# First-layernorm statistics of the next query block computed inside the output-projection loop, on VectorE, in an eight-core transformer layer

## The chip, the cores and the metric

The kernel runs on all 8 cores of one Trainium2 chip. Each core takes one half of the token groups of one of four sequences (2048 of 4096 tokens) and never speaks to another core. The metric is the device time in microseconds (us) of the slowest core.

## What is computed

One pre-norm layer on x of shape (4, 4096, 2048): attention with 16 query heads over 4 key/value heads of 128, then a gated feed-forward part of inner width 6144 with weights rounded to fp8.

```python
def _layernorm(x, axis=-1, eps=1e-5):
    m = jnp.mean(x, axis=axis, keepdims=True)
    v = jnp.var(x, axis=axis, keepdims=True)
    return (x - m) / jnp.sqrt(v + eps)
# attention, on x = layernorm(x)
q = _rmsnorm((x @ Wq).reshape(b, s, H, DH), q_gamma)
k = _rmsnorm((x @ Wk).reshape(b, s, KVH, DH), k_gamma)
v = (x @ Wv).reshape(b, s, KVH, DH)
scores = jnp.einsum('bqhd,bkhd->bhqk', q, k) * DH ** (-0.5)      # causal
out = jnp.einsum('bhqk,bkhd->bqhd', softmax(scores), v) @ Wo + x
# the layer
x = x + attention(_layernorm(x))
x = x + ffn(_layernorm(x))   # silu(x @ gate * s) * (x @ up * s) @ down * s
```

## The kernel before

Everything lies transposed: the 2048 features are 16 tiles of 128 partitions (`DC = FC = 16`), the tokens are columns, 512 at a time. The kernel has three stages. First the keys and values of all 4096 tokens are made in eight steps of 512. Then a loop over four query blocks (`for qc in range(NQC)`) does all of attention for 512 queries. Then the feed-forward part runs in two halves of 1024 tokens.

The change touches the query-block loop. One block goes through these steps:

1. **Statistics of the first layernorm** (lines 475 to 500). ScalarE copies each of the 16 feature tiles of `xtt` (fp32) to `xnn` (bf16); TensorE multiplies each by a column of ones (`ones1`) and accumulates the sum over features in row 0 of the PSUM bank `PS_G`; ScalarE then squares each tile of `xnn` in place; TensorE accumulates the squares in `PS_H`. `t_sumsq` is the semaphore count of the last matmul.
2. **Rows and normalisation** (from line 501). VectorE makes mean and variance rows, ScalarE the inverse deviation, TensorE spreads both over 128 partitions, and VectorE normalises the 16 tiles into `xnn`. The first row operation also waits for `gd["rows1"]` (line 502): the small transfers that stored the previous block's rows, since it overwrites them.
3. **Attention**, eight head pairs.
4. **Output projection** (`for fc in range(FC)`, lines 830 to 879). For each of 16 output tiles: GpSimd issues the transfer of 512 KB of `wo` into one of two buffers `wofc`, and that issue waits for the matmuls that read the buffer two steps earlier; TensorE does 16 matmuls into bank `PS_S0` or `PS_S1`; TensorE then does two statistics matmuls of the *second* layernorm for the step before (`ln2_stats(fc - 1)`), from `qraw` and `qsq`; VectorE adds the two residuals (`rlB`, then `x1t`), casts to `qraw` and squares to `qsq`; SyncE stores `x1t`, and loads the next block's tile of `xtt` over the one just used (the list `preload`), on a semaphore of its own, `X{fc}`.
5. **Rows of the second layernorm** (from line 880), which end with two small stores `rbc<-rowb` on semaphore `RW`.

Each engine takes its instructions strictly in the order in which the Python emits them, and waits are emitted by hand as counts of semaphores. `vop` and `act` also make each VectorE or ScalarE operation wait for the one before on the same engine. All operations are recorded under the line of their helper: matmuls L112, ScalarE L124, VectorE L132, transfers L93.

Of the kernel before, what the change touches and what calls it, by code (L numbers as in the profile page):

```python
# [12 lines left out]
AF = mybir.ActivationFunctionType  # L13
ALU = mybir.AluOpType
# [3 lines left out]
DC = 16  # L18
S = 4096
# [5 lines left out]
NQC = 4  # L25
# [11 lines left out]
def _build():  # L37
# [36 lines left out]
    def wait(e, c, v):  # L74
        assert v <= cnt[c], f"wait on future: {e} {c} {v} > {cnt[c]}"
        if v <= 0:
            return
        emit(e, lambda eng, s=c, v=v: eng.wait_ge(sem[s], v))

    def gwait(e, g):  # L80
        if not g:
            return
        if isinstance(g, list):
            for gg in g:
                wait(e, gg[0], gg[1])
        else:
            wait(e, g[0], g[1])
# [17 lines left out]
    def mm(o, l, r, st, sp, inc=False):  # L105
        if inc:
            cnt["T"] += 1
            emit("tensor", lambda eng, o=o, l=l, r=r, st=st, sp=sp:
                 eng.matmul(o, l, r, start=st, stop=sp).then_inc(sem["T"], 1))
            return cnt["T"]  # L110
        emit("tensor", lambda eng, o=o, l=l, r=r, st=st, sp=sp:
             eng.matmul(o, l, r, start=st, stop=sp))  # L112

    def act(o, i, f, bias=None, scale=None, inc=False):
        kw = {}
        if bias is not None:
            kw["bias"] = bias
        if scale is not None:
            kw["scale"] = scale
        if cnt["S"] > 0:  # L120
            emit("scalar", lambda eng, v=cnt["S"]: eng.wait_ge(sem["S"], v))
        cnt["S"] += 1
        emit("scalar", lambda eng, o=o, i=i, f=f, kw=kw:
             eng.activation(out=o, in_=i, func=f, **kw).then_inc(sem["S"], 1))  # L124
        return cnt["S"]
# [18 lines left out]
    def tinc():  # L144
        cnt["T"] += 1
        last = prog["tensor"].pop()
        emit("tensor", lambda eng, f=last: f(eng).then_inc(sem["T"], 1))
        return cnt["T"]
# [21 lines left out]
    with ExitStack() as TOP:  # L170
# [8 lines left out]
        ones1 = TOP.enter_context(nc.sbuf_tensor("ones1", [128, 1], BF16))  # L179
# [9 lines left out]
        def row(i):  # L189
            return rowb[0:1, i * 512:(i + 1) * 512]  # L190

        ps = [TOP.enter_context(nc.psum_tensor(f"ps{i}", [128, 512], F32))
              for i in range(4)]
# [30 lines left out]
        with ExitStack() as SA:  # L224
# [209 lines left out]
            with ExitStack() as SA2:  # L434
# [27 lines left out]
                minv2_slot = {}  # L462

                preload = [None]
                for qc in range(NQC):
                    K_QC = 8 * qc + 8
                    if preload[0] is not None:
                        xls = preload[0]
                    else:
                        xls = []  # L470
                        for dc in range(DC):
                            xls.append(dma("sync", xtt[:, dc * 512:(dc + 1) * 512],
                                           xq[:, qc * 512:(qc + 1) * 512].rearrange(
                                               "(dc p) t -> p dc t", p=128)[:, dc, :], f"X{dc}"))
                    s_cp = []
                    for dc in range(DC):
                        wait("scalar", f"X{dc}", xls[dc])
                        if dc == 0:
                            gwait("scalar", gd.get("xnn_sq"))
                        s_cp.append(act(xnn[:, dc * 512:(dc + 1) * 512],  # L480
                                        xtt[:, dc * 512:(dc + 1) * 512], AF.Copy))
                    tsx = []
                    for dc in range(DC):
                        wait("tensor", "S", s_cp[dc])
                        if dc == 0:
                            gwait("tensor", gd.get("av10"))
                            gwait("tensor", gd.get("av11"))
                        mm(ps[PS_G][0:1, :], ones1[:, :], xnn[:, dc * 512:(dc + 1) * 512],
                           dc == 0, dc == DC - 1)
                        tsx.append(tinc())  # L490
                    s_sq = []
                    for dc in range(DC):
                        wait("scalar", "T", tsx[dc])
                        s_sq.append(act(xnn[:, dc * 512:(dc + 1) * 512],
                                        xnn[:, dc * 512:(dc + 1) * 512], AF.Square))
                    for dc in range(DC):
                        wait("tensor", "S", s_sq[dc])
                        mm(ps[PS_H][0:1, :], ones1[:, :], xnn[:, dc * 512:(dc + 1) * 512],
                           dc == 0, dc == DC - 1)
                    t_sumsq = tinc()  # L500
                    wait("vector", "T", t_sumsq)
                    gwait("vector", gd.get("rows1"))
                    vop("tensor_scalar", row(R_MEAN), ps[PS_G][0:1, :], 1.0 / D, None, ALU.mult)
# [314 lines left out]
                    def ln2_stats(i):  # L818
                        wait("tensor", "V", v_x1b_of[i])
                        if i == 0:  # L820
                            gwait("tensor", gd.get("lbank0"))
                            gwait("tensor", gd.get("lbank1"))
                        mm(ps[PS_L0][0:1, :], ones1[:, :], qraw[0][:, :], i == 0, i == FC - 1)
                        mm(ps[PS_L1][0:1, :], ones1[:, :], qsq[:, :], i == 0, i == FC - 1)
                        t_st = tinc()
                        gd["qsq"] = ("T", t_st)
                        gd["qraw0"] = ("T", t_st)
                        return t_st

                    for fc in range(FC):  # L830
                        wb_ = fc % 2
                        gwait("gpsimd", gd.get(f"wofc{wb_}"))
                        wod = dma("gpsimd", wofc[wb_][:, :],
                                  wo[:, fc * 128:(fc + 1) * 128].rearrange("(dc p) f -> p dc f", p=128),
                                  f"WO{wb_}")
                        b = PS_S0 if fc % 2 == 0 else PS_S1
                        wait("tensor", f"WO{wb_}", wod)
                        if fc == 0:
                            wait("tensor", "V", v_evall)
                        gwait("tensor", gd.get(f"sbank{fc % 2}"))  # L840
                        for dc in range(DC):
                            mm(ps[b][:, :], wofc[wb_][:, dc * 128:(dc + 1) * 128],
                               attno[:, dc * 512:(dc + 1) * 512], dc == 0, dc == DC - 1)
                        t_wo = tinc()
                        if fc >= 1:
                            ln2_stats(fc - 1)
                        wait("vector", "T", t_wo)
                        gwait("vector", gd.get(f"x1t{fc % 2}"))
                        if fc == 0:
                            wores = []  # L850
                            gwait("vector", gd.get("rlB0"))
                        wores.append(vop("tensor_tensor", rlB[0][:, :], ps[b][:, :],
                                         xtt[:, fc * 512:(fc + 1) * 512], ALU.add))
                        v_x1 = vop("tensor_tensor", x1t[fc % 2][:, :], rlB[0][:, :],
                                   xnn[:, fc * 512:(fc + 1) * 512], ALU.add, inc=True)
                        gd[f"sbank{fc % 2}"] = ("V", v_x1)
                        gwait("vector", gd.get("qraw0"))
                        vop("tensor_copy", qraw[0][:, :], x1t[fc % 2][:, :])
                        gwait("vector", gd.get("qsq"))
                        v_x1b = vop("tensor_tensor", qsq[:, :], qraw[0][:, :], qraw[0][:, :],  # L860
                                    ALU.mult, inc=True)
                        v_x1b_of[fc] = v_x1b
                        wait("sync", "V", v_x1)
                        spd = dma("sync", x1s[fc, :, qc * 512:(qc + 1) * 512],
                                  x1t[fc % 2][:, :], f"SP{fc % 2}")
                        gd[f"x1t{fc % 2}"] = (f"SP{fc % 2}", spd)
                        gd[f"wofc{wb_}"] = ("T", t_wo)
                        if fc == FC - 1:
                            gd["rlB0"] = ("V", v_x1)
                        if qc < NQC - 1:  # L870
                            if fc == 0:
                                preload[0] = []
                            wait("sync", "V", wores[fc])
                            preload[0].append(dma(
                                "sync", xtt[:, fc * 512:(fc + 1) * 512],
                                xq[:, (qc + 1) * 512:(qc + 2) * 512].rearrange(
                                    "(dc p) t -> p dc t", p=128)[:, fc, :], f"X{fc}"))
                        else:
                            preload[0] = None
                    ln2_stats(FC - 1)  # L880
                    t_ln2 = cnt["T"]
                    wait("vector", "T", t_ln2)
# [280 lines left out]
```

## Time and profile before

| what | us |
|---|---|
| median of three timed runs | 6364.97 |
| the three runs | 6345.15, 6364.97, 6578.1 |
| the profiled execution | 6212.52 |
| span of its slowest core (core 7) | 6210.7 |
| spans of its eight cores | 6179.1 to 6210.7 |

The profile is of one execution, on the slowest core. Times in it are from the start of the span. An instruction's row gives start and duration; a bracket gives how long the engine was idle before it and what ended that. The granted clock of TensorE (`PEclk`) is given as a share of its full 2.4 GHz, so 0.50 is 1.2 GHz. The profiled execution is 152 us shorter than the median of the timed runs.

### The profile page before, as it was taken

How to read it: one execution, taken by the hardware profiler on the slowest of the kernel's cores; microseconds unless marked ns; L12 is line 12 of the kernel's file. 1: busy time of each engine (PE TensorE's matmuls, PEld its weight loads, DVE VectorE, ACT ScalarE, POOL GpSimd, SP SyncE). 2: the span in 40 equal slices, each digit the busy share in tenths (PEclk: the TensorE clock that was granted, in tenths of full speed). 3: DMA queues.
4: the chain of work that ended last, by engine and by line, in shares of the span. 5: the costliest groups of instructions: out<-in, count | busy, mean ns of one | idle time of the engine just before them, and what ended most of it. 6: DMA issues, size and time to landing. Idle time of an engine off the chain costs nothing.

```text
span 6210.7 us, 56932 instructions; the slowest of 8 cores (6179.1 to 6210.7 us)
## 1 busy us (share of the span) xinstructions
PE 4538.3 (73%) x16536; PEld 1582.6 (25%) x16536; DVE 1671.6 (27%) x3095; ACT 1698.6 (27%) x2511; POOL 294.1 (5%) x231
## 2 busy tenths in 40 slices
PE   4556545665666656666567777659999999999998
PEld 1112111111111211111111111224444344444443
DVE  2433334433333333333233333331110211111000
ACT  3232323321444225555145556100100000100000
POOL 0000000000000000000100000100000010000000
PEclk8666556566776868788778778879999999999999
DMA  4212121145120531010711100565566996565786
GB/s 89 55 29 53 28 48 21 21 47 75 14 28 1 81 48 14 7 14 7 109 14 14 15 7 1 75 92 39 37 41 41 112 102 53 38 41 35 52 79 70
DMA packets 670616, 271.18 MB, mean 44 GB/s; under 512 B 541286, under 2 KB 611942, under 8 KB 670318
## 3 DMA queue, kind: packets, MB, share of 16 engines
q0 software_dynamic: 598576, 147.86, 32.0%
q1 hardware_dynamic: 71742, 119.68, 7.3%
q8 instruction: 146, 2.39, 0.2%
q14 instruction: 152, 1.25, 0.1%
HBM read 532.77 MB, written 33.57 MB: 91 GB/s over the span
## 4 chain that ended last, share of the span: by engine, by line
PE 54%; ACT 17%; DVE 13%; DMA 7%; issue 7%; DVEq 1%; ACTq 1%; SPq 1%; POOLq 0%
PE ps L112 41%; PE lacc L112 13%; ACT pbt L124 9%; DMA wofc<-wo 4%; ACT xnn L124 4%; ACT rowb L124 3%; DVE pbt L132 2%; DVE rowb L132 2%; DVE xnn L132 2%; DVE xtmp L132 1%; ACT rlrow L124 1%; DVE rlB L132 1%; DMA dbuf<-dw 1%; DMA x1f<-x1s 1%; DVE outt L132 1%
## 5 line engine op out<-in xcount | busy, mean ns | idle before, releaser
L124 ACT ACTIVATE pbt<-ps,biasB,rall 128x512 bf16<-128x512 f32 x1280 | 995.0, 777 | 792.2 <-PE ps L112 419.4
L112 PE MATMUL ps<-pbt,vtok 128*128 128x512 bf16 x1280 | 598.4, 468 | 486.1 <-DVE pbt L132 241.4
L112 PE MATMUL ps<-xn,gbuf 128*128 128x512 bf16 x3072 | 699.0, 381 | 75.7 <-DVE xn L132 75.7
L112 PE MATMUL lacc<-fuse,dbuf 128*128 128x512 bf16 x3072 | 695.9, 390 | 67.4 <-DVE outt L132 58.1
L112 PE MATMUL ps<-xn,ubuf 128*128 128x512 bf16 x3072 | 694.4, 379 | 0.0
L112 PE MATMUL ps<-qhat,khat 128*128 128x512 bf16 x1280 | 609.8, 480 | 5.8 <-DVE qhat L132 5.8
L124 ACT ACTIVATE gact<-ps,gs_sb 128x512 bf16<-128x512 f32 x192 | 131.9, 687 | 1588.4 <-PE ps L112 1588.4
L132 DVE SCALAR_TENSOR_TENSOR fuse<-ps,us_sb,gact 128x512 bf16<-128x512 f32 x192 | 144.2, 751 | 1177.7 <-PE ps L112 1177.6
L112 PE MATMUL ps<-attno,wofc 128*128 128x512 bf16 x1024 | 296.8, 456 | 181.1 <-DMA wofc<-wo 169.6
L112 PEld LDWEIGHTS lacc<-fuse,dbuf 128*128 128x128 fp8e4 x3072 | 305.1, 100 | 458.1 <-issue 119.0
L132 DVE TENSOR_TENSOR pbt<-pbt 128x512 bf16<-128x512 bf16 x640 | 272.3, 426 | 544.1 <-ACT pbt L124 516.7
L112 PEld LDWEIGHTS ps<-xn,gbuf 128*128 128x128 fp8e4 x3072 | 301.6, 98 | 442.1 <-issue 82.7
L112 PEld LDWEIGHTS ps<-xn,ubuf 128*128 128x128 fp8e4 x3072 | 300.6, 98 | 362.5
L112 PEld LDWEIGHTS ps<-pbt,vtok 128*128 128x128 bf16 x1280 | 128.0, 100 | 1001.6 <-issue 981.1
L112 PE MATMUL ps<-xnn,wqhg 128*128 128x512 bf16 x1024 | 274.6, 421 | 74.3 <-DVE xnn L132 74.3
L132 DVE TENSOR_TENSOR pbt<-pbt,mask_sb 128x512 bf16<-128x512 bf16 x512 | 217.8, 425 | 305.7 <-ACT pbt L124 292.9
L112 PE MATMUL lacc<-pbt,ones 128*1 128x512 bf16 x640 | 289.5, 452 | 7.3 <-DVE pbt L132 7.2
L112 PE MATMUL ps<-xnn,wk_sb 128*128 128x512 bf16 x512 | 177.5, 477 | 148.9 <-DVE xnn L132 148.9
L124 ACT ACTIVATE rowb<-rowb,epsb 1x1 f32<-1x1 f32 (+1 forms) x80 | 30.3, 379 | 717.9 <-DVE rowb L132 717.9
L112 PE MATMUL lacc<-xnn,ones 128*1 128x512 bf16 x256 | 149.6, 584 | 83.1 <-ACT xnn L124 39.0
L112 PEld LDWEIGHTS ps<-attno,wofc 128*128 128x128 bf16 x1024 | 111.5, 113 | 365.5 <-issue 297.1
L132 DVE SCALAR_TENSOR_TENSOR outt<-lacc,ds_sb,x1g 128x512 f32<-128x512 f32 x64 | 48.1, 751 | 530.9 <-PE lacc L112 527.2
(97 smaller groups left out, 2760.1 us busy)
## 6 DMA issues: line engine op xcount, KB each, us to landing
xtt<-xT SPq DMA_DIRECT2D x128, 256.0 KB, 3.7
wqhg<-wq POOLq DMA_DIRECT2D x32, 1024.0 KB, 10.0
wofc<-wo POOLq DMA_DIRECT2D x64, 512.0 KB, 9.8
gbuf<-gw POOLq DMA_DIRECT2D x48, 512.0 KB, 9.7
ubuf<-uw POOLq DMA_DIRECT2D x48, 512.0 KB, 13.9
dbuf<-dw POOLq DMA_DIRECT2D x32, 768.0 KB, 21.5
xtt<-xq SPq DMA_DIRECT2D x64, 256.0 KB, 8.0
x1s<-x1t SPq DMA_DIRECT2D x64, 256.0 KB, 6.5
```

The costliest lines, as they stand in the source:

```text
L112: eng.matmul(o, l, r, start=st, stop=sp))
L124: eng.activation(out=o, in_=i, func=f, **kw).then_inc(sem["S"], 1))
L132: getattr(eng, n)(*a, **kw).then_inc(sem["V"], 1))
```

## The change

For query blocks 1 to 3 the statistics of the first layernorm are no longer computed at the head of the block. They are computed inside the output projection of the block before, one feature tile per step: the tile `dc = fc - 2` at step `fc` from 2 on, and tiles 14 and 15 after the loop, ahead of the last `ln2_stats`. The copy and the square move from ScalarE to VectorE. Each tile is done as one chain: VectorE copy, TensorE sum, VectorE square, TensorE sum of squares, emitted behind all else of the step. Block 0 keeps the old code.

```diff
                 preload = [None]
+                xst = {}
...
-                    s_cp = []
-                    for dc in range(DC):
-                        wait("scalar", f"X{dc}", xls[dc])
...
-                    t_sumsq = tinc()
+                    if "t_sumsq" in xst:
+                        t_sumsq = xst.pop("t_sumsq")
+                    else:
+                        (the removed lines, indented)
...
+                    def mk_xstat(dc):
+                        def fn():
+                            wait("vector", f"X{dc}", preload[0][dc])
+                            v_cp = vop("tensor_copy", xnn[:, dc * 512:(dc + 1) * 512],
+                                       xtt[:, dc * 512:(dc + 1) * 512], inc=True)
+                            wait("tensor", "V", v_cp)
+                            if dc == 0:
+                                gwait("tensor", gd.get("av10"))
+                                gwait("tensor", gd.get("av11"))
+                            mm(ps[PS_G][0:1, :], ones1[:, :],
+                               xnn[:, dc * 512:(dc + 1) * 512], dc == 0, dc == DC - 1)
+                            t_s = tinc()
+                            wait("vector", "T", t_s)
+                            v_sq = vop("tensor_tensor", xnn[:, dc * 512:(dc + 1) * 512],
+                                       xnn[:, dc * 512:(dc + 1) * 512],
+                                       xnn[:, dc * 512:(dc + 1) * 512], ALU.mult, inc=True)
+                            wait("tensor", "V", v_sq)
+                            mm(ps[PS_H][0:1, :], ones1[:, :],
+                               xnn[:, dc * 512:(dc + 1) * 512], dc == 0, dc == DC - 1)
+                            xst["t_sumsq"] = tinc()
+                        return fn
+                    xstat_cls = ([mk_xstat(dc) for dc in range(DC)]
+                                 if qc < NQC - 1 else [])
                     for fc in range(FC):
...
+                        if fc >= 2 and xstat_cls:
+                            xstat_cls.pop(0)()
+                    while xstat_cls:
+                        xstat_cls.pop(0)()
                     ln2_stats(FC - 1)
```

## Rows read from the trace of the kernel before

**Rows 1.** The page: busy time, then shares of the chain that ended last.

```profile
PE 4538.3 (73%) x16536; PEld 1582.6 (25%) x16536; DVE 1671.6 (27%) x3095; ACT 1698.6 (27%) x2511; POOL 294.1 (5%) x231
...
PE ps L112 41%; PE lacc L112 13%; ACT pbt L124 9%; DMA wofc<-wo 4%; ACT xnn L124 4%; ACT rowb L124 3%; DVE pbt L132 2%; DVE rowb L132 2%; DVE xnn L132 2%; DVE xtmp L132 1%; ACT rlrow L124 1%; DVE rlB L132 1%; DMA dbuf<-dw 1%; DMA x1f<-x1s 1%; DVE outt L132 1%
```

**Rows 2.** Windows: sum, busy us (count) of PE, PEld, DVE, ACT, POOL; PEclk, DMA, GB/s.

```profile
1346.40:1465.30 118.90, 73.75 (x252) 25.91 (x252) 29.11 (x53) 0.00 (x0) 15.99 (x14) 0.80 0.96 122
...
2092.90:2202.60 109.70, 73.03 (x252) 25.86 (x252) 29.07 (x52) 0.00 (x0) 16.18 (x14) 0.81 0.96 132
2202.60:2246.00 43.40, 20.72 (x38) 3.14 (x36) 11.76 (x18) 23.46 (x37) 0.00 (x0) 0.55 0.18 39
...
2951.50:3058.80 107.30, 70.45 (x252) 25.27 (x252) 29.09 (x53) 0.00 (x0) 16.17 (x14) 0.83 0.97 136
```

**Rows 3.** TensorE's timeline in the projection: two groups of block 1, one of block 3.

```profile
2099.54 3.63 PE L112 MATMUL ps<-attno,wofc 128*128 128x512 bf16 x16
...
2108.55 5.18 PE L112 MATMUL ps<-attno,wofc 128*128 128x512 bf16 x16 [4.86 <-DMA wofc<-wo]
...
4022.88 5.30 PE L112 MATMUL ps<-attno,wofc 128*128 128x512 bf16 x16 [3.56 <-DMA wofc<-wo]
```

**Rows 4.** The same view: three groups of block 0.

```profile
1346.41 5.66 PE L112 MATMUL ps<-attno,wofc 128*128 128x512 bf16 x16 [10.42 <-DMA wofc<-wo]
...
1382.38 6.44 PE L112 MATMUL ps<-attno,wofc 128*128 128x512 bf16 x16 [5.35 <-DMA wofc<-wo]
...
1461.41 3.61 PE L112 MATMUL ps<-attno,wofc 128*128 128x512 bf16 x16 [3.21 <-DMA wofc<-wo]
```

**Rows 5.** Chain of work in order of time, block 0: start us, us, what.

```profile
1446.88 14.28 DMA wofc<-wo
```

**Rows 6.** Timeline from the last projection matmuls of block 1 into block 2.

```profile
2199.64 2.75 PE L112 MATMUL ps<-attno,wofc 128*128 128x512 bf16 x12
...
2202.64 0.69 DVE L132 TENSOR_TENSOR rlB<-ps,xtt 128x512 f32<-128x512 f32 x1 [1.53 <-PE ps L112]
...
2204.23 0.43 DVE L132 CAST qraw<-x1t 128x512 bf16<-128x512 f32 x1
2204.61 0.38 SPq L93 DMA_DIRECT2D xtt<-xq  x1
2204.76 0.42 DVE L132 TENSOR_TENSOR qsq<-qraw 128x512 bf16<-128x512 bf16 x1
2205.33 0.38 PE L112 MATMUL lacc<-qraw,ones 128*1 128x512 bf16 x1 [2.41 <-DVE qsq L132]
2205.55 0.38 PE L112 MATMUL lacc<-qsq,ones 128*1 128x512 bf16 x1
2206.17 1.46 DVE L132 TENSOR_SCALAR rowb<-lacc 1x512 f32<-1x512 f32 x2 [0.98 <-PE lacc L112]
...
2210.88 11.44 ACT L124 ACTIVATE xnn<-xtt 128x512 bf16<-128x512 f32 x16
...
2234.91 1.46 DVE L132 TENSOR_SCALAR rowb<-ps 1x512 f32<-1x512 f32 x2 [23.27 <-PE ps L112]
```

**Rows 7.** Tile `xtt` in block 0's projection: time from issue to landing.

```profile
DMA to landing us min/median/max: 5.8/8.7/11.7
```

**Rows 8.** Timeline after the last block: rows, small stores, who waits.

```profile
4036.04 1.46 DVE L132 TENSOR_SCALAR rowb<-lacc 1x512 f32<-1x512 f32 x2 [0.98 <-PE lacc L112]
...
4043.86 1.14 POOL L93 DMA_DIRECT2D gbuf<-gw  x1 [23.37 <-DMA rbc<-rowb]
```

**Rows 9.** Windows, columns of rows 2: attention, then a wait of the projection.

```profile
1109.00:1111.50 2.50, 1.18 (x4) 0.26 (x4) 1.88 (x5) 1.55 (x3) 0.00 (x0) 1.00 0.88 88
1112.00:1116.00 4.00, 2.72 (x6) 0.42 (x6) 0.85 (x2) 1.38 (x4) 0.00 (x0) 0.50 1.16 135
...
1457.80:1461.40 3.60, 0.40 (x2) 0.02 (x1) 2.24 (x4) 0.00 (x0) 0.00 (x0) 1.00 1.29 148
```

**Rows 10.** Tile `xnn`: the statistics matmuls of the boundaries, min/median/max ns.

```profile
L112 PE MATMUL ps<-xnn,ones x128: 582/585/586, 845.6 to 3090.2; 128*1 128x512 bf16 x128
```

More of the change, by code:

```diff
@@ L474, in _build @@
                                                "(dc p) t -> p dc t", p=128)[:, dc, :], f"X{dc}"))
-                    s_cp = []
-                    for dc in range(DC):
-                        wait("scalar", f"X{dc}", xls[dc])
[L478 to L499, printed above, removed]
-                    t_sumsq = tinc()
+                    if "t_sumsq" in xst:
+                        t_sumsq = xst.pop("t_sumsq")
+                    else:
+                        s_cp = []
+                        for dc in range(DC):
+                            wait("scalar", f"X{dc}", xls[dc])
+                            if dc == 0:
+                                gwait("scalar", gd.get("xnn_sq"))
+                            s_cp.append(act(xnn[:, dc * 512:(dc + 1) * 512],
+                                            xtt[:, dc * 512:(dc + 1) * 512], AF.Copy))
+                        tsx = []
+                        for dc in range(DC):
+                            wait("tensor", "S", s_cp[dc])
+                            if dc == 0:
+                                gwait("tensor", gd.get("av10"))
+                                gwait("tensor", gd.get("av11"))
+                            mm(ps[PS_G][0:1, :], ones1[:, :], xnn[:, dc * 512:(dc + 1) * 512],
+                               dc == 0, dc == DC - 1)
+                            tsx.append(tinc())
+                        s_sq = []
+                        for dc in range(DC):
+                            wait("scalar", "T", tsx[dc])
+                            s_sq.append(act(xnn[:, dc * 512:(dc + 1) * 512],
+                                            xnn[:, dc * 512:(dc + 1) * 512], AF.Square))
+                        for dc in range(DC):
+                            wait("tensor", "S", s_sq[dc])
+                            mm(ps[PS_H][0:1, :], ones1[:, :], xnn[:, dc * 512:(dc + 1) * 512],
+                               dc == 0, dc == DC - 1)
+                        t_sumsq = tinc()
@@ L828, in ln2_stats @@
                         return t_st
+                    def mk_xstat(dc):
[4 more added lines that the diff above has]
+                            wait("tensor", "V", v_cp)
+                            if dc == 0:
+                                gwait("tensor", gd.get("av10"))
+                                gwait("tensor", gd.get("av11"))
+                            mm(ps[PS_G][0:1, :], ones1[:, :],
[12 more added lines that the diff above has]
+                                 if qc < NQC - 1 else [])
                     for fc in range(FC):
```

## The prediction

> **What bounds the kernel now.** I read the page first [rows 1]. TensorE is busy 73% of the span, and the chain that ended last runs mostly over it; the reader should note two smaller entries of that chain, the weight transfer `wofc<-wo` with 4% and ScalarE's `xnn` with 4%. The second is what the change removes for blocks 1 to 3, the first is the place where it puts the work. So the stage table comes next [rows 2]: in the projection ScalarE does nothing, VectorE is busy 29 us of 110 to 119, the DMA share is 0.96, and TensorE is busy only about two thirds. At the boundary between blocks ScalarE is the busiest engine and TensorE sees a clock of 0.55. Then the timelines: what paces the projection [rows 3 to 5], and what happens between the last projection matmul and the next block's rows [rows 6].
>
> The projection goes in pairs. Both buffers are refilled at about the same time, so two groups of 16 matmuls run back to back and then TensorE waits 3.6 to 10.4 us for weights. A group that starts after such a wait takes 5.2 to 6.4 us, since its first matmuls run at 1.2 GHz; the one behind it takes 3.63 us at 2.4 GHz [rows 3, 4]. Block by block, from the third group's first matmul to the last group's residual add, that is 118.9, 109.7 and 107.3 us for 13 steps plus one group, in sum 335.9 us [rows 2], or 8.2 to 9.1 us a step. TensorE's order of work is free of VectorE here: `ln2_stats` is one step late on purpose, so nothing waits for the add, cast and square of the same step.
>
> **What the change removes.** Copies, 32 matmuls and squares run from ScalarE's first copy at 2210.88 to VectorE's first row operation at 2234.91 [rows 6]. From the last residual add (2202.64) to that row operation it is 32.3 us; the other two boundaries have the same operations, and I price them alike.
>
> **What it adds in each step.** The new chain of a step sits in TensorE's queue ahead of the next 16 projection matmuls, and its first link sits in VectorE's queue behind the four operations of the step. So TensorE now waits each step for VectorE to work through the step just ended. From the end of a group, with durations of [rows 6]: 0.24 us to the residual add (2202.64 less the group's end at 2199.64 + 2.75); 2.54 us for add, add, cast and square (2202.64 to 2204.76 + 0.42); 0.11 us gap; the copy, priced as the cast of fp32 to bf16 of that size, 0.43; 0.15 to TensorE (2205.18 to 2205.33); matmul 0.38; 0.24 back (2205.55 + 0.38 to 2206.17); square 0.43; 0.15; and 0.22 until the next matmul can follow. Sum 4.89 us. The two new matmuls can run at the lower clock, 0.585 us each as at the boundaries [rows 10], which adds up to 0.4; I take half, so 5.1 us. Before, the two `ln2_stats` matmuls took 0.4 us at this place [rows 9]. I find no cover for this on TensorE itself: all projection matmuls stand behind it. The only cover is that TensorE was waiting for weights anyway.
>
> Are the weights still the limit? The issue for step fc+2 still goes out at the end of group fc. Landing took up to 14.3 us in block 0 [rows 5]. Until group fc+2 can start there now pass two stalls and a group, 5.1 + 5.2 + 5.1 = 15.4 us. So the transfer falls wholly under the new waits, and a step costs the stall plus the group. Its length then hangs on the clock. Between two groups TensorE has about 0.4 us of `ln2_stats`, 2.9 us of nothing, and two lone matmuls 0.8 us apart. The rows show both outcomes nearby: 3.6 us with 0.40 us of work kept the clock at 1.00, and the group behind took 3.61 us [rows 4, 9]; 3.56 and 4.86 us of waiting lost it [rows 3]; and in attention the clock fell to 0.50 though TensorE had been busy 1.18 us of the 2.5 before [rows 9]. The thin stretch here is about 5 us from dense work to dense work, on the far side of those, so I take a restart at 1.2 GHz in each step, and for the group 5.2 us, the size of the groups behind the shortest waits that lost the clock (5.18 and 5.30 [rows 3]). A step is 5.2 + 5.1 = 10.3 us. The two first groups of a block carry no chain and stay. Thirteen steps plus a group and 0.24: 139.3 us, three times 417.9, against 335.9: **82 us lost**. The bounds: with the clock held, 3.63 + 4.89 = 8.52 us a step, three times 114.6 = 343.9 us, 8 us lost; with the longest restart (6.44 [rows 4]) and both small matmuls slow, 6.44 + 5.3 = 11.7 us a step, 13 x 11.74 + 6.7 = 159.3 us, three times 478, 142 us lost.
>
> On this point the Trainium skill speaks against the change: "TensorE: Matmul & The Clock Gate", in the section on how oscillation of the clock bites real kernels, describes a kernel whose bursts of matmuls are parted by short waits and which starts every burst at the half clock. By it each group would restart slowly, as in my sum; the case that the clock holds would then be out. The trace agrees for the waits of 3.56 us and more and does not for the one of 3.21 us.
>
> **What is left at the boundary.** Chains 13, 14 and 15 follow the last group. Chain 13 and 14 end on VectorE about 6 us behind the residual add. Chain 15 needs tile 15 of `xtt`, whose load is issued 1.97 us behind the add [rows 6] and lands 8.7 us later, 5.8 to 11.7 [rows 7]. So a new wait of some 4 us stands in VectorE's queue; behind it stand the rows of both layernorms. Copy at 10.7, then 0.43 + 0.15 + 0.38 + 0.24 + 0.43 + 0.15 to the last sum of squares at 12.5, `ln2_stats(15)` 0.22 later, and 0.84 more to the first row operation (2205.33 to 2206.17): 13.6, with slow matmuls 14.0. Before it was 3.5. Next the second layernorm's rows, and behind them the wait of line 502 for the small stores, which the old statistics hid: at the end of the last block first row operation to stores landed is 7.8 us [rows 8]. The first layernorm's rows start at 14.0 + 7.8 = 21.8 us instead of 32.3: **10.5 us saved** per boundary, 32 in all. With loads at 5.8 or 11.7 us it is 40 or 23 in all. If neither the load nor the stores were in the way it would be more, but both are plain in the code. Moving work from ScalarE to VectorE costs nothing else: ScalarE has nothing else at either place, VectorE's busy share in the projection goes from a quarter to a third. The weight transfer of the next block's first heads is issued one step ahead of the loop's end and now gets more time, not less.
>
> **Sum.** 82 lost less 32 saved: 50 us slower. On the profiled execution 6212.5 + 50 = 6262.5. The median of the timed runs lies 152 us above it, and I carry the difference over: 6365 + 50 = **6415 us**, 0.8% slower.
>
> **Rivals.**
> *The clock holds.* If the two lone matmuls keep the clock at 1.00, a step is 8.52 us, 8 us are lost and 32 saved: 24 us faster, 6341 us. The 3.6 us stretch of [rows 9] speaks for it, the attention stretch against. The sign turns where a step costs 9.1 us with a group of 4.2 us (13 x 9.1 + 4.4, three times, is 335.9 + 32), less than any group behind a wait of 3.56 us or more. Chance 0.15.
> *The step is longer than I think.* Restarts of 6.44 us, or weights that land later than the 15.4 us of cover (14.28 us is near it), give 11.7 us a step: 142 lost, 23 saved, 119 us slower, 6484 us. Groups around 6 us are common after long waits, which speaks for it; that the waits here are short speaks against it. Chance 0.15.
> *The stall stays hidden and the boundary gives all it seems to.* The statistics go from the path, and only the stores remain: rows start at 3.5 + 7.8 = 11.3 instead of 32.3, 63 us faster, 6302 us. It needs TensorE's in-order queue and tile 15's load not to matter; the load alone speaks against it. Chance 0.03.
> The forecast has 0.65; 0.02 is left for what I don't see.
>
> A difference of 2%, 127 us, is about what a measurement of this kernel can tell from no change. The forecast and the clock rival are well within; of the long-step case about half would pass it. Slower by over 2%: 0.09; faster by over 2%: 0.02; within: 0.89. The range reaches to the two middle rivals, 6335 to 6485 us; the forecast's own is 6385 to 6450.
>
> **What would show it.** In the projection of blocks 0 to 2: steps even instead of paired, 10 to 10.5 us apart; the group's idle time before it ended by `xnn` or PE's own queue, no longer by `wofc<-wo`; PEclk lower than 0.80 in the windows of [rows 2]; groups of 5 to 6 us. The last block's projection unchanged. At the boundary a VectorE wait of about 4 us for `xtt<-xq`, then `rowb<-ps` about 22 us behind the last residual add, released by `rbc<-rowb`. If the groups take 3.6 us, the clock step fails; if the waits are still ended by `wofc<-wo`, the step on cover fails; if the row operation comes at 11 us, the step on tile 15 fails.

## The result and the profile after

The changed kernel's median is 6280.92 us over 33 timed runs, that of the kernel before 6276.33 us over 34. Some executions of either kernel are up to 7% longer than the others, with a lower granted clock on one half of the chip or on both, so every ratio in this document is taken from the others alone. The ratio here is **1.0068, 95% interval [1.0046, 1.009]**: the change makes the kernel slower by 0.7%, about 42 us, which is within 2%. The lines below come from the run "again" of the experiments, the same unaltered kernel; its profiled execution took 6261.22 us, 48.7 us more than that of the kernel before (6212.52).

The projection of blocks 0, 1 and 2, from the third group to the last residual add, and the boundary behind block 1; the view and its columns are those of [rows 2]:

```profile
1347.10:1488.20 141.10, 91.60 (x278) 30.22 (x278) 40.26 (x78) 0.00 (x0) 15.98 (x14) 0.82 0.76 105
2105.20:2243.90 138.70, 89.74 (x278) 29.44 (x278) 40.18 (x79) 0.00 (x0) 16.18 (x14) 0.83 0.80 113
2983.50:3123.90 140.40, 92.17 (x278) 30.18 (x278) 40.16 (x78) 0.00 (x0) 16.17 (x14) 0.81 0.85 113
2243.90:2261.30 17.40, 4.16 (x10) 0.68 (x8) 8.19 (x16) 1.35 (x2) 0.00 (x0) 0.63 0.29 58
```

Against [rows 2] the three stages are 141.1, 138.7 and 140.4 us long instead of 118.9, 109.7 and 107.3. VectorE has 11 us more to do in each, and the DMA share falls from 0.96 or 0.97 to between 0.76 and 0.85: the weights are no longer what the stage waits for. The pages' groups say the same; this is the projection's matmul group, before and then with the change, with busy time, mean ns, and the idle time before it:

```profile
L112 PE MATMUL ps<-attno,wofc 128*128 128x512 bf16 x1024 | 296.8, 456 | 181.1 <-DMA wofc<-wo 169.6
...
L112 PE MATMUL ps<-attno,wofc 128*128 128x512 bf16 x1024 | 322.4, 486 | 61.7 <-DMA wofc<-wo 53.5
```

Idle time ended by `wofc<-wo` fell from 169.6 to 53.5 us. The mean matmul went from 456 to 486 ns: more of them ran at the lower clock.

One step of block 1, the timeline of all engines. The columns are start, duration, engine, operation, idle time before and what ended it:

```profile
2131.56 0.69 DVE L132 TENSOR_TENSOR rlB<-ps,xtt 128x512 f32<-128x512 f32 x1 [5.90 <-PE ps L112]
...
2132.36 0.69 DVE L132 TENSOR_TENSOR x1t<-rlB,xnn 128x512 f32<-128x512 f32 x1
...
2133.16 0.43 DVE L132 CAST qraw<-x1t 128x512 bf16<-128x512 f32 x1
...
2133.69 0.42 DVE L132 TENSOR_TENSOR qsq<-qraw 128x512 bf16<-128x512 bf16 x1
2134.21 0.43 DVE L132 CAST xnn<-xtt 128x512 bf16<-128x512 f32 x1
2134.79 0.38 PE L112 MATMUL ps<-xnn,ones 128*1 128x512 bf16 x1 [2.94 <-DVE xnn L132]
2135.34 0.43 DVE L132 TENSOR_TENSOR xnn<-xnn 128x512 bf16<-128x512 bf16 x1 [0.70 <-PE ps L112]
2135.91 0.58 PE L112 MATMUL ps<-xnn,ones 128*1 128x512 bf16 x1 [0.75 <-DVE xnn L132]
2136.42 5.06 PE L112 MATMUL ps<-attno,wofc 128*128 128x512 bf16 x16
2141.42 0.38 PE L112 MATMUL lacc<-qraw,ones 128*1 128x512 bf16 x1
```

VectorE works through its four operations, then the copy; only then comes TensorE's first matmul, 2.94 us after its last one, then the square, and 0.75 us later the second. The group behind them has no idle time ended by weights, takes 5.06 us and not 3.63, and the next residual add starts at 2141.73, 10.17 us after this one. The granted clock of the same step, in three windows (VectorE at work, the group's start, its end):

```profile
2131.30:2134.80 3.50, 0.56 (x4) 0.08 (x3) 2.66 (x5) 0.00 (x0) 1.14 (x1) 1.00 0.04 6
2136.40:2138.00 1.60, 1.60 (x5) 0.58 (x5) 0.00 (x0) 0.00 (x0) 0.00 (x0) 0.50 1.33 220
2140.00:2141.40 1.40, 1.40 (x7) 0.49 (x5) 0.00 (x0) 0.00 (x0) 0.00 (x0) 1.00 0.81 142
```

The boundary behind block 1. These are the lines that answer to [rows 6] and [rows 8]:

```profile
2243.89 0.69 DVE L132 TENSOR_TENSOR rlB<-ps,xtt 128x512 f32<-128x512 f32 x1 [6.00 <-PE ps L112]
...
2245.86 0.38 SPq L93 DMA_DIRECT2D xtt<-xq  x1
...
2250.05 0.43 DVE L132 CAST xnn<-xtt 128x512 bf16<-128x512 f32 x1
...
2253.64 1.46 DVE L132 TENSOR_SCALAR rowb<-lacc 1x512 f32<-1x512 f32 x2 [1.83 <-PE lacc L112]
...
2259.54 0.62 SPq L93 DMA_DIRECT2D rbc<-rowb  x2
2261.28 1.46 DVE L132 TENSOR_SCALAR rowb<-ps 1x512 f32<-1x512 f32 x2 [1.81 <-DMA rbc<-rowb]
```

From the last residual add to the rows of the first layernorm it is 17.4 us instead of 32.3. The copy of tile 15 starts 4.2 us after its load was issued, and no wait stands in its bracket; the wait for the small stores is there, 1.81 us long.

### The profile page after: what moved, and what is told of

Its sections match the earlier page's. It is cut to its first block, busy times and chain, and to the rows that moved or that the text cites. A ratio compares the mean times of both kernels' runs of the same rounds, so it can differ in the third digit from the quotient of the medians.

```text
span 6662.4 us, 56929 instructions; the slowest of 8 cores (6475.6 to 6662.4 us)
## 1 busy us (share of the span) xinstructions
PE 4949.6 (74%) x16536; PEld 1684.0 (25%) x16536; DVE 1712.6 (26%) x3191; ACT 1638.2 (25%) x2415; POOL 293.9 (4%) x231
## 3 DMA queue, kind: packets, MB, share of 16 engines
q0 software_dynamic: 598576, 147.86, 30.5%
## 4 chain that ended last, share of the span: by engine, by line
PE 59%; ACT 15%; DVE 14%; issue 6%; DMA 4%; DVEq 1%; ACTq 1%; SPq 0%; POOLq 0%
PE ps L112 44%; PE lacc L112 14%; ACT pbt L124 8%; ACT rowb L124 3%; DVE xnn L132 3%; ACT xnn L124 2%; DVE pbt L132 2%; DVE rowb L132 2%; DMA wofc<-wo 1%; DVE xtmp L132 1%; ACT rlrow L124 1%; DVE rlB L132 1%; DVE qsq L132 1%; DVE outt L132 1%; DMA x1f<-x1s 1%
## 5 line engine op out<-in xcount | busy, mean ns | idle before, releaser
L112 PE MATMUL ps<-xn,gbuf 128*128 128x512 bf16 x3072 | 842.8, 437 | 76.3 <-DVE xn L132 76.3
L112 PE MATMUL lacc<-fuse,dbuf 128*128 128x512 bf16 x3072 | 812.1, 436 | 75.3 <-DVE outt L132 60.9
L112 PE MATMUL ps<-xn,ubuf 128*128 128x512 bf16 x3072 | 840.0, 436 | 0.0
L112 PEld LDWEIGHTS ps<-xn,gbuf 128*128 128x128 fp8e4 x3072 | 334.6, 109 | 551.3 <-issue 551.3
L112 PEld LDWEIGHTS lacc<-fuse,dbuf 128*128 128x128 fp8e4 x3072 | 331.7, 109 | 555.8 <-issue 522.0
L112 PEld LDWEIGHTS ps<-xn,ubuf 128*128 128x128 fp8e4 x3072 | 334.1, 109 | 472.5 <-issue 472.5
L112 PE MATMUL ps<-attno,wofc 128*128 128x512 bf16 x1024 | 327.6, 492 | 59.5 <-DMA wofc<-wo 51.5
L112 PE MATMUL ps<-xnn,ones 128*1 128x512 bf16 x128 | 59.1, 462 | 199.1 <-DVE xnn L132 166.7
```

## Where the time went, over all cores

The table is worked out from the traces of all eight cores of each kernel (differences between the starts of two VectorE operations, in us: for each block the median over the cores, then the sum over blocks 0 to 2). "Loop" runs from the second to the last residual add of a block, 14 steps, "boundary" from there to the first layernorm's first row operation, "attention" from there to the next block's first residual add. The table leaves out what lies before block 0's projection, the gap between the first two adds of a block, and block 3's projection; the stage after it is the last but one column.

```
kernel          loops   boundaries   attention 1 to 3   last stage   median span
before          344.6      97.2          2125.6           2176.6       6192.5
again           436.3      56.4          2126.7           2178.0       6246.3
late            346.2      61.2          2119.5           2178.2       6153.6
late_tail       348.0      50.4          2120.4           2179.2       6149.0
late_ln2        351.9      35.3          2124.9           2176.6       6127.5
act_chain       351.2      62.3          2123.3           2178.1       6162.1
fill            377.4      61.7          2123.0           2186.4       6202.9
stall           357.9      97.5          2128.3           2178.7       6205.6
tail            440.2      49.5          2126.2           2174.9       6239.1
```

"Last stage" is from block 3's last residual add to the end. For the change the ledger closes: 91.7 us lost in the loops, 40.8 saved at the boundaries, 50.9 in all, and the median span over the cores grew by 53.8. Attention and the feed-forward part did not move by more than 1.5 us. On the slowest cores, 7 before and 3 in again, the loops took 361.8 and 443.1 us: core 7 had the longest loops of the eight before, so the loss there is 81 us and not 92.

## The experiments

**again.** The changed kernel unaltered.

> The changed kernel unaltered, for a profile of an undisturbed execution. The theory of the prediction (TensorE waits each step for VectorE, weights fall under that wait, every group restarts at 1.2 GHz): steps of 10.2 to 10.3 us in the projections of blocks 0 to 2, 139 us from the third group to the last residual add, 21.8 us from there to the next block's rows; 40 to 50 us slower than before. A rival, that the loss comes from elsewhere (transfers, attention): steps near 8.5 us and the loss in another stage.

Ratio 1.0082 [1.0057, 1.0106]. On core 3, from the start of one group to the next, 30 of the 39 steps from the third groups on take 10.1 to 10.2 us, the longest 12.0; the three blocks together take 420.2 us from the third group on, against 335.9 before: the loss is in the loop and nowhere else. The boundary took less than expected, 17.3 to 19.8 us on this core.

**late.** TensorE no longer waits inside the step; VectorE does the same work at the same places, but no longer waits for TensorE's sum before it squares. The edit in short:

```diff
-    wait("tensor", "V", v_cp);  mm(PS_G, xnn[dc])
-    wait("vector", "T", t_s);   square xnn[dc] in place
-    wait("tensor", "V", v_sq);  mm(PS_H, xnn[dc])
+    vop square: qraw[1] <- xnn[dc] * xnn[dc]
+    # one step later, right behind ln2_stats(fc - 1):
+    wait("tensor", "V", v_sq);  mm(PS_G, xnn[dc]);  mm(PS_H, qraw[1])
```

> VectorE does the same copies and squares at the same places (the square goes to a free buffer instead of in place), but TensorE's two matmuls of a tile are emitted one step later, next to ln2_stats. If TensorE's wait for VectorE is the whole cost: the projection is as before (107 to 119 us from third group to last residual add, waits ended by wofc<-wo), the boundary stays near 21.8 us instead of 32.3, and the kernel is about 32 us faster than before (0.995) and 75 to 80 us faster than the change. If VectorE's extra work or its use of memory slows the weights: it stays slower than before.

Ratio 0.9964 [0.9932, 0.9996], faster than before, and 73 us faster than the change by the two ratios. The loops are back at 346 us (344.6 before) with all of VectorE's extra work in them, and the boundary keeps most of its gain (61.2 us against 56.4). TensorE's timeline in block 1:

```profile
2092.13 6.35 PE L112 MATMUL ps<-attno,wofc 128*128 128x512 bf16 x16 [5.04 <-DMA wofc<-wo]
2098.41 0.38 PE L112 MATMUL lacc<-qraw,ones 128*1 128x512 bf16 x1
2098.62 0.38 PE L112 MATMUL lacc<-qsq,ones 128*1 128x512 bf16 x1
2098.84 0.38 PE L112 MATMUL ps<-xnn,ones 128*1 128x512 bf16 x1
2099.05 0.38 PE L112 MATMUL ps<-qraw,ones 128*1 128x512 bf16 x1
2099.36 3.63 PE L112 MATMUL ps<-attno,wofc 128*128 128x512 bf16 x16
```

The pairs are back, the four small matmuls stand side by side, and the wait is for weights again. So VectorE's load and its memory traffic together cost no more than 2 us here: what cost 90 us is that TensorE's two matmuls stood in its queue where they waited for VectorE's work of the same step.

**act_chain.** The change with copy and square on ScalarE, in place, with TensorE's order unaltered. The edit in short (the waits are cut; ScalarE also waits for the residual add that read the tile):

```diff
-    v_cp = vop("tensor_copy", xnn[dc], xtt[dc])
+    s_cp = act(xnn[dc], xtt[dc], AF.Copy)      # ScalarE, queue empty
-    v_sq = vop("tensor_tensor", xnn[dc], xnn[dc], xnn[dc], ALU.mult)
+    s_sq = act(xnn[dc], xnn[dc], AF.Square)
```

> The changed kernel with copy and square of the chain on ScalarE, in place as before, at the same places in TensorE's order. ScalarE has an empty queue there, so the copy is done while the group runs and TensorE waits only for one square: about 0.38 + 0.24 + 0.63 + 0.15 + 0.22 = 1.6 us a step instead of 4.9. If the position behind VectorE's four operations is what costs: the stall is covered by the weights, the projection is as before (107 to 119 us), about 30 us faster than before. If any wait of TensorE inside the step costs its full length: 13 x 1.6 x 3 = 62 us lost against before's projection, and 30 us slower than before in all.

Ratio 0.994 [0.9918, 0.9961]. The loops take 351.2 us, 7 more than before and 85 less than the change, though TensorE still waits for a square inside every step. Block 0:

```profile
1360.69 3.61 PE L112 MATMUL ps<-attno,wofc 128*128 128x512 bf16 x16 [2.18 <-DMA wofc<-wo]
1367.07 3.61 PE L112 MATMUL ps<-attno,wofc 128*128 128x512 bf16 x16 [0.71 <-DMA wofc<-wo]
```

The groups still wait for weights behind the chain: a stall of about 1.6 us, shorter than most waits for weights before, cost 7 us over 42 steps. late says that the wait inside the step is what costs, and this kernel that most of that wait came from the chain's place behind VectorE's four operations.

**stall.** The kernel before, with one wait of TensorE added in each step and no statistics moved.

```diff
+    if fc >= 2:                       # blocks 0 to 2, end of the step
+        wait("tensor", "V", v_x1b)
```

> The kernel before with one wait added and nothing else: in blocks 0 to 2, from step 2 on, TensorE waits for VectorE's fourth operation of the same step before it goes on, 0.24 + 2.54 + 0.15 = 2.9 us behind the end of a group. By the theory that the weights cover a stall up to the wait that they caused before, and that a step is the longer of the two: group 5.2 + 2.9 = 8.1 us at most, so the projection stays at 107 to 119 us a block and the kernel within 10 us of before. A rival, that each stall adds its full length: 39 steps x 2.9 = 113 us slower.

Ratio 0.9993 [0.9938, 1.0048]; the loops grew by 13.3 us, the median span by 13.1, a little over the 10 that I had allowed. TensorE in block 1:

```profile
2108.30 3.61 PE L112 MATMUL ps<-attno,wofc 128*128 128x512 bf16 x16 [2.63 <-DVE qsq L132]
...
2139.98 3.61 PE L112 MATMUL ps<-attno,wofc 128*128 128x512 bf16 x16 [3.47 <-DMA wofc<-wo]
...
2146.98 5.30 PE L112 MATMUL ps<-attno,wofc 128*128 128x512 bf16 x16 [2.86 <-DMA wofc<-wo]
...
2155.43 5.12 PE L112 MATMUL ps<-attno,wofc 128*128 128x512 bf16 x16 [2.63 <-DVE qsq L132]
```

39 stalls of 2.9 us ahead of a group are 113 us of waiting, and 13 show up in the time. Some steps wait for VectorE and others for weights, whichever is later.

**fill.** The change, with 12 matmuls of no use in TensorE's queue ahead of each chain of the loop.

```diff
     if fc >= 2 and xstat_cls:
+        for _ in range(12):
+            mm(ps[PS_C][:, :], attno[:, 0:128], attno[:, 0:512], True, True)
         xstat_cls.pop(0)()
```

> The changed kernel with 12 extra matmuls (128x512, into a bank that nobody reads, their result is not used) in TensorE's queue ahead of each chain of the loop, 12 x 0.216 = 2.6 us of the 3 us that TensorE stands there. If the restart at 1.2 GHz is what makes a step 10.2 us: the granted clock stays at 1.00 in the projections of blocks 0 to 2, groups take 3.63 us, a step 8.5 us, 114.6 us instead of 138 from third group to last residual add, some 65 us faster than the change in spite of more work, and about 0.996 of before. If the group's length has another cause (weights, memory), a step stays at 10.2 us or more.

A stretch of block 1, with the columns of [rows 2], and one step:

```profile
2089.00:2200.00 111.00, 97.88 (x416) 36.61 (x416) 39.76 (x78) 0.00 (x0) 15.04 (x13) 1.00 0.99 127
```

```profile
2144.90 2.76 PE L112 MATMUL ps<-attno 128*128 128x512 bf16 x12
2147.91 0.38 PE L112 MATMUL ps<-xnn,ones 128*1 128x512 bf16 x1 [0.25 <-DVE xnn L132]
2149.03 0.38 PE L112 MATMUL ps<-xnn,ones 128*1 128x512 bf16 x1 [0.75 <-DVE xnn L132]
2149.34 3.63 PE L112 MATMUL ps<-attno,wofc 128*128 128x512 bf16 x16
```

In this stretch the clock is 1.00 all through, each group takes 3.63 us, and a step is 8.53 us (2140.81 to 2149.34). So the 1.7 us by which a step of the change is longer is the restart at 1.2 GHz, as the forecast had it. The loops take 59 us less than in the change, with 504 matmuls more. The total is less clear: 1.002 [0.9962, 1.0078] of before, where 0.996 was expected, just outside the interval, while the change's own 1.0068 lies inside it. So it is the trace that shows the gain, and the ratio alone does not. With steps this short the weights are late again in the last steps of blocks 0 and 2 (TensorE waits 4.2 and 4.7 us for them), and this execution's last stage was 7 to 11 us longer than in the others, for which I have no cause.

**tail.** The change, with tile 15's chain behind the second layernorm's rows.

```diff
-    while xstat_cls:
+    while len(xstat_cls) > 1:
         xstat_cls.pop(0)()
     ln2_stats(FC - 1)
     ...                               # rows of the second layernorm, stores
+    if xstat_cls:
+        xstat_cls.pop(0)()
```

> The changed kernel, with tile 15's chain moved behind the rows and small stores of the second layernorm; the loop is as in the change. By the theory of the boundary (tile 15's load and the stores are both on the path, one behind the other): rows of the first layernorm start about 13 us behind the last residual add instead of about 21, 20 to 26 us faster than the change, ratio to before 1.003 to 1.005. If one of the two is not on the path: less than half of that.

The boundaries take 49.5 us instead of 56.4, 7 us in all and not 20 to 26. A repeat beside other kernels gave the ratio:

> Repeat of the changed kernel with tile 15's chain moved, which has no ratio yet. Its profile shows the first layernorm's rows 16.5 us behind the last residual add against 18.7 in the change: 3 x 2.1 = 6 us faster than the change, 1.007 of before.

It was 1.0069 [1.0043, 1.0096], as expected, and not to be told from the change itself. In the timeline of tail, block 0, the last residual add starts at 1488.90:

```profile
1497.00 1.46 DVE L132 TENSOR_SCALAR rowb<-lacc 1x512 f32<-1x512 f32 x2 [1.83 <-PE lacc L112]
...
1502.57 0.43 DVE L132 CAST xnn<-xtt 128x512 bf16<-128x512 f32 x1
...
1505.38 1.46 DVE L132 TENSOR_SCALAR rowb<-ps 1x512 f32<-1x512 f32 x2 [1.05 <-PE ps L112]
```

The second layernorm's rows start 8.1 us behind the add, since chains 13 and 14 stand ahead of them, and take 5.6 us; tile 15's copy follows without a wait, its load long landed, and its chain adds 2.8 us. The expected 13 us left out that the rows and this chain stand one behind the other in VectorE's queue.

**late_tail.** Late matmuls and tile 15 moved as in tail.

> As the kernel with late matmuls, and tile 15's copy, square and matmuls are emitted behind the rows of the second layernorm, so that these rows and their small stores pass while tile 15 of xtt is still on its way. If tile 15's load and the stores are what is left at the boundary: rows of the first layernorm start about 13 us behind the last residual add instead of 21.8, some 57 us faster than before (0.991), 25 us faster than with late matmuls alone. If they are not, no gain over it.

Ratio 0.9917 [0.9902, 0.9932]. A repeat:

> Repeat of late matmuls with tile 15 moved, beside the next variant on one chip: 0.990 to 0.993 of before, as measured.

It gave 0.9941 [0.9917, 0.9964], a little outside what the first had led me to expect. The boundaries took 50.4 and 52.4 us, so rows start near 17 us, not 13; over late alone it gained 9 to 11 us there, not 25. The load of tile 15 is out of the way here, but at 16 of the 24 boundaries of the eight cores VectorE now waits for the load of tile 14, ahead of the rows, for up to 5.9 us.

**late_ln2.** Late matmuls, and the second layernorm's rows with their stores moved from the boundary to behind the next block's normalisation.

```diff
-    (rows of the second layernorm, two stores, at the end of block qc)
+    (the same lines, in block qc + 1, behind the 16 normalised tiles,
+     ahead of the first query projection; block 3 keeps them in place)
```

> As the kernel with late matmuls, and in blocks 0 to 2 the rows of the second layernorm with their small stores are moved from ahead of the next block's first rows to behind its normalisation. The rows then stand in nobody's way at the boundary, and the stores have all of attention to land. If the 7.3 us of rows and stores are on the path: first layernorm rows start about 12.5 us behind the last residual add (tile 15's load and its chain), 7 us earlier than with late matmuls alone and 4 us earlier than with tile 15 moved; up to 3 us come back as VectorE time ahead of the first query heads. 10 to 20 us faster than late matmuls alone, ratio to before about 0.990.

Ratio **0.9903 [0.9886, 0.9921]**, the fastest kernel of the study, by the ratios about 60 us faster than before and 102 faster than the change. Boundaries: 11.0, 13.0 and 11.3 us; attention gave back 5 us of it over late. What is left in block 1 is the loads of tile 14 (first line) and tile 15 (second), which are waited for here since the two last groups run back to back and the loads are issued only 4.7 us apart:

```profile
2180.92 0.43 DVE L132 CAST xnn<-xtt 128x512 bf16<-128x512 f32 x1 [4.12 <-DMA xtt<-xq]
...
2183.16 0.43 DVE L132 CAST xnn<-xtt 128x512 bf16<-128x512 f32 x1 [1.27 <-DMA xtt<-xq]
...
2185.59 1.47 DVE L132 TENSOR_SCALAR rowb<-ps 1x512 f32<-1x512 f32 x2 [1.47 <-PE ps L112]
```

## Why the prediction was right or wrong

*The wait in TensorE's queue: right, and so was its size.* I had put 4.89 to 5.1 us behind each group. The step shown above is 10.17 us with a group of 5.06, so 5.1 us; its parts 2.94, 0.38 and 0.75 us stand where the sum had them. late shows that the wait itself, not VectorE's work, is the cost.

*The weights fall under it: right.* Idle time ended by weights went from 169.6 to 53.5 us, of which 30.5 us are in block 3, whose code is unchanged, and 22.3 us in front of the three third groups. The cover was closer than the sum had it: the 14.3 us of [rows 5] are one piece of the chain, and from issue to landing the transfers of block 0's projection took up to 15.7 us before, more than the 15.4 us of cover. With the change they took 8.1 to 14.9 us there, and the one of 14.9 made the last group of block 0 wait 0.78 us. The rule used, that a step costs the longer of the two, is what stall and act_chain measured: 2.9 us of added stall cost 0.3 us a step, 1.6 us cost 0.2.

*The clock restarts in each step: right.* Step forecast 10.3 us, measured 10.2; the three blocks 417.9 forecast, 420.2 measured on core 3. None of the 312 groups from the fourth on, over all eight cores, took less than 4.6 us. One sign that I had named failed: PEclk in the windows is 0.82, 0.83 and 0.81, and not lower than the 0.80 to 0.83 of before. The mean over a window counts the waits too, and in the step shown the granted clock was 1.00 while TensorE had little to do and 0.50 only from about the group's start. The length of the group is the better sign. fill removed the restart and the step fell to 8.53 us, where the clock rival had 8.52. That rival and the one that the stall stays hidden are out, as is the long step.

*Tile 15's load: a term too dear, most of 8.8 us in all.* I took 8.7 us from issue to landing, the median of all 16 loads of block 0 [rows 7]. It is one load that counts, the last, and on core 7 it lands sooner than the median. The same view narrowed to that one issue gives, for block 1, before the change

```profile
DMA to landing us min/median/max: 5.8/5.8/5.8
```

and with it

```profile
DMA to landing us min/median/max: 4.0/4.0/4.0
```

For blocks 0 and 2 it is 5.8 and 6.5 us before, 6.8 and 4.3 with the change. So a narrower look at core 7 would have given 5.8 to 6.5. Other cores differ: the medians over all eight are 7.3, 7.7 and 6.8 us before, 6.3, 5.2 and 5.8 with the change, and 7.4, 8.2 and 7.6 in late, where the weights come as densely as before. That goes with the other traffic: in the 4.2 us behind the issue the DMA share was 1.08 before and 0.54 in the change in block 1; that this is the cause was not isolated by a run. In place of the 4 us that I forecast, VectorE waited for tile 15 between 0 and 2.9 us, with a median of 1.8 over three blocks and eight cores, and not at all in block 1 of core 3. Each boundary took 18.8 us instead of 21.8, and 40.8 us were saved and not 32. The experiments tail and late_tail missed for other reasons, given with them.

*The small stores: right.* 1.81 us of wait, and 7.3 to 7.6 us from row operation to row operation where I had 7.8.

*The sum: right as a difference, wrong as a time.* 82 lost and 32 saved, 50 us, against 91.7 and 40.8 over the cores, 50.9 (the two are counted from the second add here, from the third group there), 48.7 us between the two profiled executions, and about 42 us in the ratio. Part of this closeness is luck: the 335.9 us that I compared with belong to core 7, the longest of the eight (317.1 to 335.8 us), so the median loss was 10 us larger than forecast, and the saving was larger by nearly as much.

What failed is the step that carried the profiled execution to the median, "152 us above it, and I carry the difference over". I took the median of three runs, 6365 us, for the level of the kernel before. All three were above what this kernel mostly takes: over 34 runs its median is 6276 us, 89 us lower, and 18 of the 34 lie between 6199 and 6283 us, as does the profiled execution at 6212.5 us. The sum against the profiled execution gave 6262.5 us, and the profiled execution of the changed kernel took 6261.22 us; its median over 33 runs is 6280.92 us, where I had 6415. My own working held a sign of it: with 6345, 6365 and 6578 us beside a profiled 6212, the level was the least certain number of the text, and the range had no term for it.

## What to carry to other kernels

Before moving work into a loop, find where its instructions stand in the in-order queue of the engine that paces the loop. A link that waits for another engine's work of the *same* step exposes that engine's whole queue; the same link emitted one step later cost 2 us in 42 steps, and here that alone is the difference between 0.8% slower and 0.4% faster. A stall is paid for the most part only beyond the wait that is already there, but if it parts two bursts of matmuls, price the second burst at the lower clock. Where one load decides, read the landing of that load, on more than one core, and not the median of its kind. And before a difference is added to a level, ask how well the level is known: three runs were not enough here.

## What the runs showed of the hardware

TensorE's clock fell in waits as short as some that had kept it. In stall, waits of 2.63 us were followed by groups of 3.61 us at 2108.30 and of 5.12 us at 2155.43, one of 2.86 us by 5.30 us, and one of 3.47 us by 3.61 us. The length of the wait before a group does not settle by itself whether the group starts at 1.2 GHz. In the change, where 2.94 and 0.75 us of waiting stand around single small matmuls in every step, no group from the fourth on kept the full clock.
